# Adaptive-LayerNorm attention block on one core: the second batch is normalised by ScalarE, five heads are rotated in one piece, query weights are loaded ahead of the fourth modulation

## The chip, the cores and the metric

The kernel runs on one core of one Trainium2 chip. The metric is the device time of one launch in microseconds (us), as the median of several runs. The abbreviations are those of the profile: PE is TensorE, PEld its weight loads, DVE VectorE, ACT ScalarE, POOL GpSimd, SP SyncE, which issues nearly all DMAs. PEclk is the share of its full clock of 2.4 GHz that the throttle granted to TensorE.

## What is computed

```python
def reference(x, wq, wk, wv, wo, w12, b12, w3, b3, c, wmod):      # x: 2 x 512 x 512, 32 heads, 8 key/value heads of 128
    mod = (_silu(c) @ wmod).reshape(2, 6, 1, -1)
    sa, ca, ga, sb, cb, gb = (mod[:, 0], mod[:, 1], mod[:, 2], mod[:, 3], mod[:, 4], mod[:, 5])
    ga = (2 * (ga >= 0) - 1) * jnp.maximum(jnp.abs(ga), 0.25)
    gb = (2 * (gb >= 0) - 1) * jnp.maximum(jnp.abs(gb), 0.25)
    h = _layernorm(x, axis=-1) * (1 + ca) + sa
    x = x + ga * attention(h, wq, wk, wv, wo)      # rotary embedding on q and k, causal softmax, 4 query heads to a key head
    h = _layernorm(x, axis=-1) * (1 + cb) + sb
    return x + gb * ffn(h, w12, b12, w3, b3)       # silu(x1) * x2, then the second matrix
```

## The kernel before

Five instruction streams, one for each engine, are written out by hand. Each engine works its own stream strictly in order, and semaphores join them (`x.wait_ge(sem, n)` before an instruction, `.then_inc(sem, 1)` after one). So the order in which a function writes its calls is the order of the engine, and a waiting instruction holds up all that stands behind it.

All products are made with fp32 operands that are split into a high and a low part: one product of 128 x 512 is three matmuls per chunk of the contraction, and a projection with its four chunks is 12 matmuls (`product`, `project_k`, `project_v`, `project_q`). ACT makes the high part, POOL or DVE the low one. That holds for weights (`wq_high`, then `wq_low`), for the normalised input (`hT`), and for rotated queries and keys.

**Main part.** It has 8 key heads x 2 batches. `group` is one key head, of eight slots `s`; a slot is 128 query rows. In a slot TensorE makes the scores (four products of growing width), a query projection for a later slot (`slot_query`, into `q_bank`), sometimes a key or value projection into `x_bank`, the product of probabilities and values (`attend`) and the output product (`project_out`). DVE takes the row maxima, ACT the exponentials, DVE the reciprocal of the sums (`invert`), ACT the scaling (`normalise`), DVE the 32 x 32 transposes (`turn_blocks`), and two DMAs through DRAM lay the probabilities out for `attend`. In the first group the modulations 4, 5 and 2, which are long rows of matmuls of two columns (`modulation`), stand behind the scores of slots 1 and 2.

**Rotation.** For each projected head DVE makes two rows of products with the cosine and sine tables (`rotate`, three instructions that read the PSUM bank, then `roped`), POOL adds them (`rotated_sum`), ACT makes the high part (`rotated_high`), POOL the low part (`rotated_low`, then `rope_lo`). There are two buffers (`rope_tmp[:, n % 2]`), so rotation n waits for `rope_lo` of rotation n - 2. The first scores wait for `rope_lo` of rotations 0 (key) to 4 (query head 3); the first `slot_query` waits until rotation 5 (query head 0 of batch 1) has left its bank: `ROPE_FIRST` is 6.

**Prologue**, which the change touches. SP loads x, the two halves of modulations 0 and 1, key and query weights and the tables. TensorE makes modulations 0 and 1 as rows, and in between turns the normalised x of batch 0 into `s_banks` (`turn_x(0)`). ACT scales and shifts it (`modulate_x`), DVE splits it (`hT`), and TensorE projects key head 0 and the query heads. Batch 1 follows: DVE makes mean and reciprocal deviation (`norm_scale`, a chain of 12 instructions on 128 x 4 elements), and before the change also the normalised rows (`norm_x`, four instructions of 128 x 512); TensorE turns them (`turn_x(1)`), ACT modulates them and makes the high part, DVE the low part (`h_low`). Before the change modulation 3 stands on TensorE between the query heads 1 and 2, the norm of batch 1 on DVE between rotations, and the projection of query head 0 of batch 1 ahead of the first scores.

## Time and profile before

| | us |
|---|---|
| median of 3 runs (lowest, highest) | 840.23 (840.01, 843.87) |
| the profiled execution, its own time | 841.05 |
| its span, first to last instruction | 839.2 |
| PE busy | 790.2 (94%) |
| DVE busy | 615.1 (73%) |
| POOL busy | 560.1 (67%) |
| ACT busy | 501.9 (60%) |
| mean granted clock of TensorE | 0.969 |

A busy share is a mean over the whole span; what a change at one place is worth is read from the chain of waits there. Times in the trace count from the first instruction. Granted clock 1.00 is 2.4 GHz, 0.50 is 1.2 GHz; a stretch in between holds both.

### The profile page before, as it was taken

Reading aid. Unit: us, or ns where it says so; the run is one execution under the profiler, and the core shown is the slowest. Engines: PE = TensorE matmul, PEld = TensorE weight load, DVE = VectorE, ACT = ScalarE, POOL = GpSimd, SP = SyncE. Lnnn points to the kernel's source line nnn. Section 1 sums busy time; section 2 is a strip of 40 time slices with the busy share of each in tenths; the row PEclk is TensorE's granted clock in tenths of the full one; section 3 lists DMA queues with packets and bytes.
Section 4 is the critical chain, followed back from the end, with each engine's and each line's share of the span. In section 5 each row is a group of like instructions: output and inputs, shape, how many; then the busy total and the mean of one; then the engine's idle time right before and its main releaser. Section 6 shows DMA issues by size and latency. Waiting matters only on the chain.

```text
span 839.2 us, 11685 instructions
## 1 busy us (share of the span) xinstructions
PE 790.2 (94%) x3680; PEld 653.8 (78%) x3680; DVE 615.1 (73%) x1246; ACT 501.9 (60%) x1191; POOL 560.1 (67%) x374
## 2 busy tenths in 40 slices
PE   7989989989999999999999999999999987889887
PEld 2769868877888888888888888888888776668765
DVE  5856467867777878687768676867787778558695
ACT  2154476557667766776677667777667754853421
POOL 1453395768777877796779677989587974148552
PEclk9788799999999999999999999999999998999999
DMA  9512646677667756776676667776676854966011
GB/s 326 191 39 69 205 128 167 137 175 238 154 189 192 230 147 198 191 218 172 183 196 202 180 181 194 236 190 174 176 219 177 244 157 128 310 205 192 0 51 50
DMA packets 191885, 147.13 MB, mean 175 GB/s; under 512 B 62673, under 2 KB 168273, under 8 KB 189777
## 3 DMA queue, kind: packets, MB, share of 16 engines
q1 hardware_dynamic: 191408, 146.33, 62.3%
q8 instruction: 29, 0.48, 0.2%
q14 instruction: 32, 0.25, 0.1%
q10 hardware_dynamic: 416, 0.07, 0.0%
HBM read 91.82 MB, written 54.53 MB: 174 GB/s over the span
## 4 chain that ended last, share of the span: by engine, by line
PE 53%; POOL 13%; DVE 12%; ACT 8%; DMA 7%; SPq 4%; issue 3%; DVEq 0%; ACTq 0%; POOLq 0%
PE out_bank L571 13%; PE q_bank L504 13%; PE s_bank L504 8%; PE o_bank L557 7%; PE x_bank L504 6%; DMA spread_dram<-turned 5%; POOL pT_lo L1340 5%; POOL wo_lo_sb L1340 3%; ACT probs L1137 3%; POOL rope_tmp L1366 2%; ACT probs L1145 2%; PE o_bank L512 2%; POOL qT L1340 2%; DVE turned L827 2%; SPq L395 1%
## 5 line engine op out<-in xcount | busy, mean ns | idle before, releaser
L1340 POOL TENSOR_TENSOR pT_lo<-pT_raw,pT_hi 128x1024 fp32r<-128x1024 f32 (+1 forms) x96 | 194.7, 2043 | 87.2 <-ACT pT_hi L1114 87.2
L1137 ACT ACTIVATE probs<-probs,neg_max 128x32 f32<-128x32 f32 (+15 forms) x256 | 130.7, 512 | 181.2 <-DVE neg_max L808 181.2
L1340 POOL TENSOR_TENSOR qT<-rope_tmp,qT 128x512 fp32r<-128x512 f32 x64 | 83.3, 1301 | 101.3 <-ACT qT L1114 101.3
L827 DVE STREAM_TRANSPOSE turned<-probs 128x512 f32<-128x512 f32 (+1 forms) x64 | 96.7, 1512 | 50.5 <-DMA spread_dram<-turned 43.9
L1366 POOL TENSOR_TENSOR rope_tmp<-rope_tmp 128x512 f32<-128x512 f32 x80 | 109.3, 1373 | 29.3 <-DVE rope_tmp L785 29.3
L504 PE MATMUL s_bank<-kT,qT 128*128 128x32 f32 (+15 forms) x768 | 123.4, 309 | 4.4 <-POOL qT L1340 4.4
L504 PEld LDWEIGHTS s_bank<-kT,qT 128*128 128x128 f32 x768 | 114.5, 192 | 12.9 <-issue 4.1
L571 PE MATMUL out_bank<-wo_hi_sb,attn_hi 128*128 128x512 f32 x248 | 99.4, 401 | 15.2 <-POOL wo_lo_sb L1340 6.8
L1145 ACT ACTIVATE probs<-probs,row_inv 128x32 f32<-128x32 f32 (+15 forms) x256 | 111.9, 509 | 0.8 <-DVE row_inv L817 0.8
L808 DVE CUSTOM_DVE_ANT_0 probs<-s_bank,mask_sb 128x32 f32<-128x32 f32 (+15 forms) x256 | 98.5, 433 | 17.0 <-PE s_bank L504 16.8
L504 PE MATMUL q_bank<-hT_hi,wq_hi_sb 128*128 128x512 f32 x248 | 101.6, 410 | 1.1 <-DVE rope_tmp L785 1.0
L504 PE MATMUL q_bank<-hT_hi,wq_lo_sb 128*128 128x512 f32 x248 | 100.4, 405 | 0.0
L504 PE MATMUL q_bank<-hT_lo,wq_hi_sb 128*128 128x512 f32 x248 | 100.2, 404 | 0.0
L571 PE MATMUL out_bank<-wo_lo_sb,attn_hi 128*128 128x512 f32 x248 | 97.9, 395 | 0.0
L571 PE MATMUL out_bank<-wo_hi_sb,attn_lo 128*128 128x512 f32 x248 | 97.7, 394 | 0.0
L783 DVE TENSOR_TENSOR rope_tmp<-q_bank,cos_sb 128x512 f32<-128x512 f32 x62 | 42.5, 686 | 63.8 <-PE q_bank L504 32.6
L1114 ACT ACTIVATE pT_hi<-pT_raw 128x1024 fp32r<-128x1024 f32 (+1 forms) x96 | 83.6, 903 | 6.3 <-DMA pT_raw<-spread_dram 6.0
L557 PE MATMUL o_bank<-pT_hi,v_hi 128*128 128x512 f32 x160 | 63.7, 398 | 9.6 <-DVE attn_lo L831 8.0
L571 PEld LDWEIGHTS out_bank<-wo_hi_sb,attn_hi 128*128 128x128 f32 x248 | 47.5, 191 | 30.2 <-issue 13.4
L1340 POOL TENSOR_TENSOR wq_lo_sb<-wq_raw,wq_hi_sb 128x512 fp32r<-128x512 f32 x40 | 52.0, 1300 | 23.7 <-ACT wq_hi_sb L1114 23.7
L557 PE MATMUL o_bank<-pT_lo,v_hi 128*128 128x512 f32 x160 | 63.2, 395 | 0.0
L557 PE MATMUL o_bank<-pT_hi,v_lo 128*128 128x512 f32 x160 | 63.2, 395 | 0.0
(218 smaller groups left out, 1612.6 us busy)
## 6 DMA issues: line engine op xcount, KB each, us to landing
spread_dram<-turned SPq DMA_DIRECT2D x64, 256.0 KB, 4.1
pT_raw<-spread_dram SPq DMA_DIRECT2D x16, 1024.0 KB, 5.8
spread_dram<-turned SPq DMA_DIRECT2D x64, 192.0 KB, 5.2
pT_raw<-spread_dram SPq DMA_DIRECT2D x16, 768.0 KB, 5.0
wq_raw<-in_L_attn_wq_dram SPq DMA_DIRECT2D x36, 256.0 KB, 4.3
wo_raw<-in_L_attn_wo_dram SPq DMA_DIRECT2D x9, 1024.0 KB, 5.7
spread_dram<-turned SPq DMA_DIRECT2D x64, 128.0 KB, 4.2
pT_raw<-spread_dram SPq DMA_DIRECT2D x16, 512.0 KB, 6.0
```

Of the source, the lines that this page charges most:

```text
L504: last = pe.matmul(dst, lhs(a, cc), rhs(b, cc), start=(k == 0), stop=(k == len(todo) - 1))
L512: last = pe.matmul(o_bank[:, at:at + 2], wmod_blocks[m][:, k, n * P:(n + 1) * P], c_silu[:, :, k], start=(k == 0), stop=(k == KC - 1))
L557: last = pe.matmul(o_bank[:, :], v_s[a][:, b, st_, :], pT[bb][par][:, :, PLACES[par] - 1 - i + st_, :], start=(k == 0), stop=(k == len(ste ...
L571: last = pe.matmul(dst[:, :], attn[a][:, s % 2, h * P:(h + 1) * P], wo_s[bb][:, h, :], start=(h == 0 and (a, bb) == PARTS[0]), stop=(h == ...
L783: nc.vector.tensor_tensor(a, src[:, :], cos_sb[:, :], ALU.mult)
L808: nc.vector.tensor_tensor_reduce(prob_rows(s, t), s_banks[t][:, 0:n].rearrange("p (j s) -> p j s", s=W32), mask_sb[:, T - n:T].rearrange(" ...
L827: nc.vector.transpose(dst, src).then_inc(blocks_turned, 1)
L1114: nc.scalar.activation(dst, src, ACT.Copy).then_inc(done, 1)
L1137: nc.scalar.activation(rows, rows, ACT.Exp, bias=neg_max[:, par, t:t + 1], scale=-1.0, accum_out=row_sum[:, par, t:t + 1]).then_inc(exp_do ...
L1145: last = nc.scalar.activation(rows, rows, ACT.Copy, scale=row_inv[:, par, t:t + 1])
L1340: nc.gpsimd.tensor_tensor(dst, src, hi.bitcast(f32), ALU.subtract).then_inc(done, 1)
L1366: nc.gpsimd.tensor_tensor(a, a, b, ALU.add).then_inc(rope_sum, 1)
```

## The change

1. The norm of batch 1: `norm_scale` moves on DVE to directly behind its statistics, ahead of the split of batch 0; the four `norm_x` instructions go from DVE to ACT (as an Identity activation with scale `rstd` and bias `shift`).
2. The copy of modulations 0 and 1 out of PSUM goes from DVE to ACT.
3. SP loads query heads 1, 2, 3 and the value weights before modulation 3.
4. TensorE: `turn_x(1)` comes behind query head 1, then query heads 2 and 3, the value projection, then modulation 3. Query head 0 of batch 1 is projected into `out_bank` behind the first scores.
5. DVE: rotations 0 to 4 in one piece, then the low parts of batch 1. Rotation 5 stands in slot 0 behind `turn_blocks`.
6. ACT normalises slot 0 directly behind its exponentials; batch 1 is modulated in two pairs around the high part of rotation 2. POOL makes all weights' low parts first, then the rotations in order.

```diff
@@ SP
-            load_wq(0, 1)
+            for h in range(1, REP):
+                load_wq(0, h)
+            load_wv(0)
             load_wmod(3)
-            load_wq(0, 2)
-            load_wv(0)
-            load_wq(0, 3)
@@ TensorE, group
                     scores(g, s)
+                    if first and s == 0:
+                        pe.wait_ge(roped, 5)
+                        project_q(out_bank[:, :], 1, 0, h_lo[1])
...
-                        project_k(batch_of(v), h_lo[1] if first and s == 0 else None)
+                        project_k(batch_of(v))
@@ TensorE, prologue
             project_q(out_bank[:, :], 0, 1)
-            pe.wait_ge(mod_ready, 1)
-            modulation(3)
+            pe.wait_ge(x_normed[1], TT)
+            turn_x(1, range(KC))
             pe.wait_ge(roped, 2)
             pe.wait_ge(wq_lo, 3)
             project_q(q_bank[:, :], 0, 2)
-            pe.wait_ge(x_normed, B * TT)
-            turn_x(1, range(KC))
-            pe.wait_ge(wv_lo, 1)
-            project_v(0)
             pe.wait_ge(roped, 3)
             pe.wait_ge(wq_lo, 4)
             project_q(out_bank[:, :], 0, 3)
-            pe.wait_ge(roped, 4)
-            project_q(q_bank[:, :], 1, 0, h_lo[1])
+            pe.wait_ge(wv_lo, 1)
+            project_v(0)
+            pe.wait_ge(mod_ready, 2)
+            modulation(3)
             pe.wait_ge(h_ready[1], KC)
@@ DVE, group
                     invert(g, s)
+                    if first and s == 0:
+                        turn_blocks(g, s)
+                        first_rotation(ROPE_FIRST - 1)
@@ DVE, prologue
-            dve.wait_ge(mod_made, 2)
-            link(nc.vector.tensor_copy(mod[:, 0:2 * KC, :]..., o_bank[:, 0:4 * KC]))
-            nc.vector.tensor_scalar(one_plus[:, 0:KC, :], ...).then_inc(mod_ready, 1)
+            norm_scale(1, 2)
...
-            first_rotation(0)
-            norm_scale(1, 2)
-            first_rotation(1)
-            norm_x(1)
-            first_rotation(2)
-            first_rotation(3)
+            for n in range(ROPE_FIRST - 1):
+                first_rotation(n)
             for k in range(KC):
                 h_low(k)
-            first_rotation(4)
@@ ACT, prologue
-            act.wait_ge(mod_ready, 1)
+            act.wait_ge(mod_made, 2)
+            nc.scalar.activation(mod[:, 0:2 * KC, :]..., o_bank[:, 0:4 * KC], ACT.Copy).then_inc(mod_ready, 1)
+            nc.scalar.activation(one_plus[:, 0:KC, :]..., o_bank[:, 2 * KC:4 * KC], ACT.Copy, bias=1.0).then_inc(mod_ready, 1)
+            act.wait_ge(mod_ready, 2)
             for k in range(KC):
                 modulate_x(0, k)
             wq_high(0, 1)
+            act.wait_ge(norm_ready, 2)
+            for w in range(TT, 2 * TT):
+                nc.scalar.activation(acc[:, w, :], acc[:, w, :], ACT.Identity, bias=shift[:, w, :],
+                                     scale=rstd[:, w, :]).then_inc(x_normed[1], 1)
```

On **TensorE** around the first scores the order was this (the last matmul of query head 0 of batch 1, the scores, the first of the first slot query):

```order
L504 MATMUL q_bank<-hT_hi,wq_lo_sb 128x512
L504 MATMUL s_bank<-kT,qT 128x32 [waits rope_lo,h_ready1]
L504 MATMUL s_bank<-kT,qT 128x32 x2
L504 MATMUL s_bank<-kT,qT 128x64 x3
L504 MATMUL s_bank<-kT,qT 128x96 x3
L504 MATMUL s_bank<-kT,qT 128x128 x3
L504 MATMUL q_bank<-hT_hi,wq_hi_sb 128x512 [waits wq_lo,roped]
```

and is now this:

```order
L511 MATMUL o_bank<-c_silu,wmod_sb 128x2 [waits wmod_in3,mod_ready]
L511 MATMUL o_bank<-c_silu,wmod_sb 128x2 x15
L503 MATMUL s_bank<-kT,qT 128x32 [waits rope_lo,h_ready1]
L503 MATMUL s_bank<-kT,qT 128x32 x2
L503 MATMUL s_bank<-kT,qT 128x64 x3
L503 MATMUL s_bank<-kT,qT 128x96 x3
L503 MATMUL s_bank<-kT,qT 128x128 x3
L503 MATMUL out_bank<-hT_hi,wq_hi_sb 128x512 [waits h_lo1,roped]
...
L503 MATMUL q_bank<-hT_hi,wq_hi_sb 128x512 [waits wq_lo,roped]
```

Modulation 3 has come to stand directly ahead of the scores, and the projection of head 0 of batch 1 between the scores and the first slot query, whose wait for `roped` is unchanged.

On **DVE** behind the key's rotation (`x_bank`) the order was this:

```order
L785 TENSOR_TENSOR rope_tmp<-x_bank,sin_sb 64x512
L949 BN_AGGR moments<-stats 128x2 [waits stats_made]
L949 BN_AGGR moments<-stats 128x2 x3
L957 TENSOR_SCALAR var_eps<-moments 128x4 [waits moments_ready]
...
L963 SCALAR_TENSOR_TENSOR shift<-moments,rstd 128x4 [waits dve_chain]
L783 TENSOR_TENSOR rope_tmp<-q_bank,cos_sb 128x512 [waits q_proj]
L784 TENSOR_TENSOR rope_tmp<-q_bank,sin_sb 64x512
L785 TENSOR_TENSOR rope_tmp<-q_bank,sin_sb 64x512
L1004 TENSOR_SCALAR acc<-acc,moments,rstd 128x512 x4
L783 TENSOR_TENSOR rope_tmp<-out_bank,cos_sb 128x512 [waits rope_lo,q_proj]
```

and is now this:

```order
L785 TENSOR_TENSOR rope_tmp<-x_bank,sin_sb 64x512
L783 TENSOR_TENSOR rope_tmp<-q_bank,cos_sb 128x512 [waits q_proj]
L784 TENSOR_TENSOR rope_tmp<-q_bank,sin_sb 64x512
L785 TENSOR_TENSOR rope_tmp<-q_bank,sin_sb 64x512
L783 TENSOR_TENSOR rope_tmp<-out_bank,cos_sb 128x512 [waits rope_lo,q_proj]
```

The chain of the norm and the four wide instructions no longer stand between rotations.

On DVE **in slot 0** of the first group, from the reciprocal of the row sums on, the change gives:

```order
L817 RECIPROCAL row_inv<-row_sum 128x4 [waits exp_done]
L827 STREAM_TRANSPOSE turned<-probs 128x4x128 [waits probs_normed]
L783 TENSOR_TENSOR rope_tmp<-out_bank,cos_sb 128x512 [waits rope_lo,q_proj]
L784 TENSOR_TENSOR rope_tmp<-out_bank,sin_sb 64x512
L785 TENSOR_TENSOR rope_tmp<-out_bank,sin_sb 64x512
L783 TENSOR_TENSOR rope_tmp<-q_bank,cos_sb 128x512 [waits rope_lo,q_proj]
```

Before, rotation 5 stood ahead of the row maxima of this slot, and the transpose behind the rotation of `q_bank`. Now rotation 5, for which the slot query on TensorE waits, has maxima, reciprocal and transpose ahead of it.

## Rows read from the trace of the kernel before

**Rows 1.** Busy time by stretch: us, PE, PEld, DVE, ACT, POOL busy, granted clock, DMA.

```profile
0.00:58.47 58.47, 47.08 (x192) 31.79 (x193) 42.16 (x97) 18.05 (x33) 22.82 (x21) 0.89 0.58 192
58.47:66.14 7.67, 7.67 (x26) 6.13 (x26) 2.96 (x7) 2.89 (x10) 1.65 (x2) 0.70 0.20 59
66.14:101.60 35.46, 35.46 (x181) 32.29 (x180) 17.17 (x43) 14.80 (x40) 14.07 (x11) 0.76 0.50 145
```

**Rows 2.** The chain of waits, 26 to 67 us: start, duration, what.

```profile
26.73 0.69 DVE rope_tmp L783
...
36.52 3.72 DVE acc L1004 x4
...
53.92 0.64 ACT qT L1114
...
54.62 1.27 POOL qT L1340
...
56.03 2.64 PE s_bank L504 x12
58.67 4.88 PE q_bank L504 x12
63.56 2.74 PE x_bank L504 x12
```

**Rows 3.** Timeline of DVE, norm of batch 1: start, duration, engine, line, instruction, tiles.

```profile
29.27 0.95 DVE L957 TENSOR_SCALAR var_eps<-moments 128x4 f32<-128x4 f32 x1
...
32.74 0.16 DVE L961 SCALAR_TENSOR_TENSOR newton<-newton,var_eps 128x4 f32<-128x4 f32 x1
```

**Rows 4.** Timeline of DVE, norm of batch 0.

```profile
10.56 1.91 DVE L1004 TENSOR_SCALAR acc<-acc,moments,rstd 128x512 f32<-128x512 f32 x4
```

**Rows 5.** Timeline of ACT, norm of the second layer late in the kernel.

```profile
784.58 2.94 ACT L1197 ACTIVATE rope_tmp<-acc,shift,rstd 128x512 f32<-128x512 f32 x4 [5.94 <-DVE shift L963]
```

**Rows 6.** Timeline of POOL and DVE around the split of batch 0.

```profile
17.41 1.26 POOL L1340 TENSOR_TENSOR wq_lo_sb<-wq_raw,wq_hi_sb 128x512 fp32r<-128x512 f32 x1
...
19.81 0.43 DVE L1022 CAST hT_hi<-probs 128x512 fp32r<-128x512 f32 x1 [0.85 <-ACT probs L1180]
```

**Rows 7.** Busy time by stretch: transposes, idle PE, modulations, what followed.

```profile
13.00:15.00 2.00, 2.00 (x18) 1.79 (x18) 0.44 (x1) 0.00 (x0) 0.00 (x0) 1.00 1.13 324
18.60:21.60 3.00, 0.00 (x0) 0.00 (x0) 1.88 (x6) 2.60 (x4) 0.06 (x1) 1.00 1.09 351
...
31.90:35.50 3.60, 3.60 (x33) 3.54 (x31) 3.28 (x12) 0.00 (x0) 0.78 (x1) 1.00 0.17 15
36.50:41.80 5.30, 5.26 (x12) 4.02 (x13) 5.26 (x7) 1.67 (x3) 4.29 (x3) 0.50 0.00 0
...
52.30:56.00 3.70, 0.01 (x1) 0.00 (x0) 3.33 (x11) 0.72 (x2) 2.64 (x3) 1.00 0.29 70
56.00:62.80 6.80, 6.77 (x22) 5.88 (x23) 1.18 (x9) 3.87 (x14) 2.39 (x2) 0.51 0.28 81
...
73.50:76.40 2.90, 2.90 (x8) 2.31 (x7) 0.00 (x0) 2.81 (x6) 2.09 (x2) 0.50 0.00 0
...
80.50:89.40 8.90, 8.90 (x43) 8.90 (x44) 1.97 (x10) 5.43 (x16) 3.42 (x3) 0.50 0.74 174
...
104.00:120.00 16.00, 13.32 (x61) 10.63 (x61) 11.97 (x23) 10.68 (x26) 15.39 (x9) 1.00 0.63 185
```

**Rows 8.** Timeline of PE in slot 4 of the first group.

```profile
114.98 0.47 PE L571 MATMUL out_bank<-wo_hi_sb,attn_hi 128*128 128x512 f32 x1 [2.02 <-POOL wo_lo_sb L1340]
```

**Rows 9.** Timeline, rotation and softmax of slot 0.

```profile
41.07 0.69 DVE L784 TENSOR_TENSOR rope_tmp<-out_bank,sin_sb 64x512 f32<-64x512 f32 x1
...
59.97 1.10 ACT L1145 ACTIVATE probs<-probs,row_inv 128x32 f32<-128x32 f32 x4
...
65.72 0.71 DVE L827 STREAM_TRANSPOSE turned<-probs 128x512 f32<-128x512 f32 x1
```

**Rows 10.** Groups by line, 26 to 56 us: count, busy us, mean ns, idle before.

```profile
L991 DVE TENSOR_TENSOR hT_lo<-turned,hT_hi 128x512 fp32r<-128x512 f32 x4 | 3.7, 948 | 2.2 <-ACT hT_hi L1114 2.2
```

More of the change, by code:

```diff
@@ L173, in adaln_block @@
         stats_made, moments_ready, norm_ready = sem("stats_made"), sem("moments_ready"), sem("norm_ready")
-        x_normed, x_turned = sem("x_normed"), sem("x_turned")
+        x_normed, x_turned = [sem(f"x_normed{b}") for b in range(B)], sem("x_turned")
         h_ready, h_hi, h_lo = ([sem(f"h_{s}{b}") for b in range(B)] for s in ("ready", "hi", "lo"))
@@ L677, in _ @@
             pe.wait_ge(ident_in, 16)
[L678 removed]
+            pe.wait_ge(x_normed[0], TT)
             turn_x(0, range(KC))
@@ L876, in group @@
                             wo_low(LOAD[v - 1], n)
-                    turn_blocks(g, s)
+                    if not (first and s == 0):
+                        turn_blocks(g, s)
                     if r == 0:
@@ L1000, in _ @@
             nc.vector.tensor_tensor(c_silu[:, :, :], c_silu[:, :, :], cT[:, :, :], ALU.mult).then_inc(c_ready, 1)
-            def norm_x(b):
-                for w in range(TT * b, TT * (b + 1)):
-                    nc.vector.tensor_scalar(acc[:, w, :], acc[:, w, :], moments[:, w, 0:1], rstd[:, w, :],
-                                            ALU.subtract, ALU.mult).then_inc(x_normed, 1)
             for w in range(TT):
@@ L1011, in _ @@
             norm_scale(0, 1)
-            norm_x(0)
+            for w in range(TT):
+                nc.vector.tensor_scalar(acc[:, w, :], acc[:, w, :], moments[:, w, 0:1], rstd[:, w, :],
+                                        ALU.subtract, ALU.mult).then_inc(x_normed[0], 1)
             dve.wait_ge(x_in[2], 16)
@@ L1203, in group @@
                     exponents(g, s)
+                    if first and s == 0:
+                        normalise(g, s)
                     q_high(g, s - 1)
@@ L1210, in group @@
                             wo_high(LOAD[v - 1], n)
-                    normalise(g, s)
+                    if not (first and s == 0):
+                        normalise(g, s)
                     if first and s == 3:
@@ L1284, in _ @@
             copy_rows(1)
-            act.wait_ge(mod_ready, 1)
+            act.wait_ge(mod_made, 2)
+            nc.scalar.activation(mod[:, 0:2 * KC, :].rearrange("p m b -> p (m b)"), o_bank[:, 0:4 * KC],
+                                 ACT.Copy).then_inc(mod_ready, 1)
+            nc.scalar.activation(one_plus[:, 0:KC, :].rearrange("p m b -> p (m b)"), o_bank[:, 2 * KC:4 * KC],
+                                 ACT.Copy, bias=1.0).then_inc(mod_ready, 1)
+            act.wait_ge(mod_ready, 2)
             for k in range(KC):
@@ L1288, in _ @@
             wq_high(0, 1)
+            act.wait_ge(norm_ready, 2)
+            for w in range(TT, 2 * TT):
+                nc.scalar.activation(acc[:, w, :], acc[:, w, :], ACT.Identity, bias=shift[:, w, :],
+                                     scale=rstd[:, w, :]).then_inc(x_normed[1], 1)
             wq_high(0, 2)
+            wq_high(0, 3)
+            wv_high(0)
             rotated_high(0, 0, kT[0][0][:, :])
             rotated_high(0, 1, qT[0][0][:, :, 0, :])
-            wv_high(0)
-            wq_high(0, 3)
+            modulate_x(1, 0)
+            modulate_x(1, 1)
             rotated_high(0, 2, qT[0][0][:, :, 1, :])
-            for k in range(KC):
-                modulate_x(1, k)
+            modulate_x(1, 2)
+            modulate_x(1, 3)
             rotated_high(0, 3, qT[0][0][:, :, 2, :])
@@ L1450, in _ @@
             wk_low(0)
-            wq_low(0, 0)
-            wq_low(0, 1)
+            for h in range(REP):
+                wq_low(0, h)
+            wv_low(0)
             rotated_sum(0, 0)
-            wq_low(0, 2)
             rotated_low(0, 0, kT[0][0][:, :], kT[1][0][:, :])
-            rotated_sum(0, 1)
-            rotated_low(0, 1, qT[0][0][:, :, 0, :], qT[1][0][:, :, 0, :])
-            wv_low(0)
-            rotated_sum(0, 2)
-            wq_low(0, 3)
-            rotated_low(0, 2, qT[0][0][:, :, 1, :], qT[1][0][:, :, 1, :])
-            for n in range(3, 5):
+            for n in range(1, ROPE_FIRST - 1):
                 rotated_sum(0, n)
                 rotated_low(0, n, qT[0][0][:, :, n - 1, :], qT[1][0][:, :, n - 1, :])
-            rotated_sum(0, 5)
+            rotated_sum(0, ROPE_FIRST - 1)
             def x4_low(u):
```

6 lines of the change are left out of this document (1 added, 5 removed).

## The prediction

> **What bounds the kernel now.** I read first the busy time by stretch, to see how the prologue divides [rows 1]. From 58.47 us, the start of the first slot query, to 101.60 TensorE is never idle: 7.67 of 7.67 and 35.46 of 35.46 us busy, at a clock of 0.70 and 0.76. In the 58.47 us before it is idle for 11.4 us. So what the change does ahead of 58.47 arrives at the end through one number, the time at which the first slot query starts, and a second one, the clock at which TensorE works from there. Behind 101.60 all waits are between engines, none on a fixed time, and the whole stream shifts.
>
> The chain of waits tells what sets 58.47 [rows 2]. It runs over DVE: the first rotation at 26.73, the four wide instructions of the norm of batch 1 (3.72 us on the chain), then rotations, and over ACT and POOL for the last query head (0.64 and 1.27 us) to the scores at 56.03. TensorE does the scores in 2.64 us and the slot query in 4.88, against 2.74 for the key projection behind it, also 12 matmuls. The difference, 2.14 us, is the clock: 0.51 in the stretch from 56.00 to 62.80 [rows 7].
>
> The timelines give the prices. A small instruction of the norm chain takes 0.16 us alone and 0.95 where a POOL instruction runs [rows 3]. The four wide ones took 1.91 us for batch 0, with POOL idle [rows 4], and 3.72 on the chain for batch 1 [rows 2]. ACT normalises four rows of the same size in 2.94 us [rows 5].
>
> **The change, part by part.** I follow the new order from the split of batch 0.
>
> *Norm chain moved forward on DVE.* It now starts when the statistics are done, near 17.0 us, and its first small instruction meets POOL's 17.41 to 18.67 [rows 6]; then 12 at some 0.2 us with their gaps: 21.0. The split of batch 0 started at 19.81 [rows 6], so it is 1.2 us late. Part of it comes back, since the same split waited for POOL once anyway and ACT's modulation will then be ahead. Bounds for the end of the key projection are 0 and 1.2 us late; I take 0.6, as neither end is nearer: its rotation starts at 27.3 instead of 26.73. ACT takes over two copies of modulations, which cost what DVE's did: nothing.
>
> *Norm on ACT.* 2.94 us [rows 5], from 22.5 to about 25.5, under the projections of key and query head 0. Its cover is the time until `turn_x(1)` at 32.7; seven us are left. The weights' high parts wait behind it, query head 2's until 26, used at 34.7. *Loads reordered:* query and value weights come earlier, modulation 3's megabyte later, but it is used 11 us later: nothing either way.
>
> *TensorE's own work.* From 27.3: query heads 0 and 1, 2 x 2.74; transposes 2.0 [rows 7]; heads 2 and 3 and the value projection, 3 x 2.74; modulation 3, 3.6 [rows 7]. That is 13.7 + 2.0 + 3.6 = 19.3 us, so 46.6, if nothing stalls it and the clock stays at 2.4 GHz.
>
> *The rotations.* Head 3 is projected at 40.2. Its rotation is 3 x 0.69 = 2.1 us [rows 9], to 42.3. POOL needs 1.27 for the sum, ACT 0.64, POOL 1.27, with handoffs 3.3: 45.6 if POOL is free. But POOL must first make sum and low part of head 2, to about 43.0, and shares the time with DVE's four low parts, which took 3.7 us for four with POOL beside them, where 2.8 would do at 0.69 each [rows 10, 9]. So the last low part lands at 43.0 + 3.3 + 1.0 = 47.3. This is behind TensorE's 46.6, so **the scores start at 47.3** instead of 56.03, 8.7 us earlier. Bounds: 46.6 and 49.5.
>
> The Trainium skill (SBUF — State Buffer, "Who interferes with whom") says that a Vector instruction with two SBUF inputs and a GpSimd one exclude each other for their whole length. Rows 3 agree. By that rule the four low parts could put up to 4 x 0.69 = 2.8 us between POOL's instructions where I put 1.0; the scores would start at 49.1 and the sum below would gain 1.8 us less.
>
> *Query head 0 of batch 1 behind the scores.* This is the price of the change. The first slot query still waits for rotation 5, and rotation 5 now stands behind maxima, reciprocal and transpose. Modulation 3 now directly precedes the scores; before, the stretch behind it ran at 0.50 [rows 7], and the scores took 2.64 us at that level [rows 2]. I take the same: scores end at 49.9. From the end of the scores to ACT's scaling there were 59.97 - 58.67 = 1.3 us, the scaling takes 1.10, the transpose 0.71 [rows 9]: 53.0. TensorE meanwhile projects head 0 of batch 1: at 1.2 GHz 4.9 us, at 2.4 GHz 2.74. Low stretches behind such a place lasted some 6.8 us [rows 7], so the level rises near 54: the head ends at 54.7. It ends last, not the softmax. Rotation 5: 2.1. **The first slot query starts at 56.9**, 1.6 us before 58.47, of the 8.7 that had been won. TensorE is idle from 54.7 to 56.9 for it.
>
> *Clock behind it.* The slot query took 4.88 us at 0.51. If the level is 2.4 GHz by then, it takes 2.74: 2.14 less. An idle of 2.02 us on TensorE [rows 8] did not lower the level, 1.00 in its stretch; idles of 3.0 and 3.7 us did [rows 7]. The 2.2 us here are nearest to the first. So I take 2.14.
>
> **Sum.** 1.6 + 2.1 = 3.7 us. Against the profiled execution, 841.05, that is 837.35; it stands 0.8 above the median, so the forecast for the median of 840.23 is **836.5 us**. 0.5% of it, 4.2 us, is about what a measurement of this kernel can tell from no change; the border is 836.0.
>
> **The rivals.**
>
> *B, the clock falls at the new idle.* The 2.2 us at 54.7 to 56.9 do what 3.0 us did [rows 7]. The slot query then takes 4.9 us again: the gain is 1.6 and the time 838.6. For it: idle of that length lies between the two cases that rows show, and the transition may come at another point of the program in each execution. Against: rows 8.
>
> *C, the clock does not fall at the scores.* Before, TensorE was idle 1 us behind modulation 3; now 0.7 at most. Scores take 1.5 us, the head 2.74; rotation 5 then follows the softmax, at 54.3 or so, and the slot query starts 1.8 us sooner: 834.7. Against: the fall behind the other modulations too, with no idle at all (0.50 from 73.50 and from 80.50) [rows 7].
>
> *D, transposes.* The Trainium skill (TensorE: Matmul & The Clock Gate, Part 4, "PE-mode transpose") says that transposes do not count as work that keeps the clock up. The row from 13 to 15 us is 16 transposes at 1.00 [rows 7], though the clock may have been about to fall. As a mechanism of this kernel: `turn_x(1)` now stands between projections, query head 2 and part of head 3 run at 1.2 GHz, and 1.7 us (half of a low stretch such as the one around 73.50 to 76.40) is lost on a path where 0.7 us is slack; DVE's and POOL's chain hangs on the same heads, so 1.7 us less is won: 838.2.
>
> *E, slower than before.* The level falls at the idle as in B and is still 1.2 GHz when modulation 4 begins, near 66 us. Modulation 4 then runs as the later ones did, 43 matmuls in 8.9 us, 0.21 each [rows 7], so 6.8 for 32 instead of 3.5: 3.3 lost. Key projection and the next query head run low in part, 3 more. From B's 838.6 that gives 844.9. It decides from the point at which the level is low when modulation 4 starts; before, it had risen at 62.8, 5.8 us ahead. Against: dense projections have always brought it back before [rows 1, 7].
>
> *F, nothing arrives.* The scores start late (49.5, the upper bound) and the clock falls as in B; or the loads do hold something. 840.0.
>
> **How the numbers follow.** A, the forecast, 0.45; B 0.20; C 0.14; D 0.05; E 0.07; F 0.09. A has its own width: bounds of the key projection (-0.6 to +0.6) and of the scores' start (-0.7 to +2.2) give 835.2 to 838.7. Below 836.0 lie C, a third of A and the best of B and D, where modulations 4, 5 and 2 happen to lose less clock: 0.14 + 0.16 + 0.05 = 0.35. Over 844.4 lies most of E: 0.06. Between: 0.59. The range has to reach C at the low end, less its outermost, and F at the other: 833.8 to 840.6 leaves out E, part of C and of F, near 0.18.
>
> **What would show it.** In the changed profile: the norm chain of batch 1 at 17 to 21 us, the key's rotation from 27.3; ACT's four normalising instructions of 0.73 us each; TensorE without idle from 27 to 46.6; the first scores at 47.3 (46.6 to 49.5) with a clock near 0.5; head 0 of batch 1 ending at 54.7, then some 2.2 us idle on TensorE, released by DVE's rotation; the slot query at 56.9 and of 2.74 us; slot 1's scores starting near 62.4 instead of 66.14. The forecast is wrong if TensorE's busy stretch does not begin earlier, if it begins before 55, or if the clock between it and 101.60, shifted, differs from 0.76: then the phases of modulations 4, 5 and 2 decide, not the prologue.

## The result, and the profile after

| | before | after |
|---|---|---|
| median of 20 runs each, on the same chips (lowest, highest) | 841.69 (836.95, 844.52) | 836.84 (833.23, 840.01) |
| the profiled execution, its own time | 841.05 | 836.97 |
| its span | 839.2 | 834.4 |
| PE busy | 790.2 | 789.0 |
| DVE busy | 615.1 | 609.1 |
| ACT busy | 501.9 | 505.0 |
| POOL busy | 560.1 | 560.0 |
| mean granted clock | 0.969 | 0.970 |

The ratio of the runs is 0.9946, 95% interval 0.9932 to 0.9961: 3.3 to 5.7 us less, 4.9 between the medians. The predicted time of 836.5 is met within 0.4 us. Part of that is luck: the forecast took 3.7 us off the 840.23 of three runs, and twenty runs put the kernel before at 841.69, so 4.9 were won and not 3.7. The way there is another one too, and that is what the rest is about. A single execution far above its kernel at a clock far below it (one of 982.64 us at 0.743, for example) is left out of all figures.

Busy time by stretch of the changed kernel, from the three borders of [rows 1] at the same matmuls (start of the first slot query, of slot 1's scores, and the matmul that stood at 101.60), and then the low stretches. Columns as in rows 1: stretch, us, busy of PE, PEld, DVE, ACT, POOL, granted clock, DMA share, GB/s.

```profile
0.00:59.87 59.87, 49.90 (x193) 33.62 (x193) 38.72 (x95) 23.01 (x46) 21.44 (x20) 0.86 0.60 194
59.87:67.04 7.17, 7.17 (x25) 5.76 (x25) 2.06 (x3) 1.15 (x2) 3.13 (x3) 0.76 0.28 77
67.04:99.30 32.26, 32.26 (x182) 29.34 (x181) 16.97 (x42) 14.83 (x41) 13.86 (x11) 0.84 0.48 143
24.00:30.80 6.80, 6.08 (x15) 4.48 (x15) 3.95 (x7) 3.18 (x6) 4.17 (x4) 0.52 1.05 387
47.90:58.10 10.20, 9.78 (x33) 8.09 (x33) 5.28 (x20) 2.83 (x12) 1.45 (x1) 0.52 0.20 52
61.60:65.00 3.40, 3.40 (x11) 2.65 (x9) 0.69 (x2) 0.76 (x2) 1.27 (x1) 0.56 0.02 5
82.10:92.30 10.20, 10.20 (x37) 9.03 (x37) 0.32 (x2) 4.12 (x12) 2.53 (x2) 0.52 0.88 264
```

The first slot query starts at 59.87, 1.4 us **later** than the 58.47 of before, and slot 1's scores at 67.04 instead of 66.14. At 99.30 the kernel is ahead, by 2.3 us: the stretch from slot 1's scores took 32.26 us instead of 35.46, at a clock of 0.84 instead of 0.76, and with the same matmuls. So in this execution the prologue brings no earlier start of slot 1.

The chain of waits of the changed kernel, 25 to 67 us (start, duration, what), against [rows 2]:

```profile
25.12 4.21 PE x_bank L503 x9
29.32 3.34 PE q_bank L503 x12
...
37.14 2.74 PE q_bank L503 x12
39.87 2.72 PE out_bank L503 x12
...
45.31 4.48 PE o_bank L511 x32
49.80 2.66 PE s_bank L503 x12
52.46 5.24 PE out_bank L503 x12
...
59.87 4.39 PE q_bank L503 x12
64.25 2.94 PE x_bank L503 x12
```

From 25 us to 57.7 the chain is TensorE's own work, as the new order wants. The scores come 6.4 us earlier (49.66 against 56.03 on the timeline), but head 0 of batch 1 behind them takes 5.24 us, at half clock, then rotation 5 is waited for, and the slot query takes 4.39. The timeline of DVE (start, duration, engine, line, instruction, idle before and its releaser):

```profile
18.38 1.21 DVE L961 TENSOR_SCALAR var_eps<-moments 128x4 f32<-128x4 f32 x1
...
22.95 1.51 DVE L1021 CAST hT_hi<-probs 128x512 fp32r<-128x512 f32 x1
...
29.44 0.69 DVE L783 TENSOR_TENSOR rope_tmp<-x_bank,cos_sb 128x512 f32<-128x512 f32 x1 [2.83 <-PE x_bank L503]
...
44.76 5.14 DVE L995 TENSOR_TENSOR hT_lo<-turned,hT_hi 128x512 fp32r<-128x512 f32 x4
```

The timeline of ACT:

```profile
22.69 2.93 ACT L1292 ACTIVATE acc<-acc,shift,rstd 128x512 f32<-128x512 f32 x4
```

The timeline of POOL:

```profile
18.30 1.26 POOL L1347 TENSOR_TENSOR wq_lo_sb<-wq_raw,wq_hi_sb 128x512 fp32r<-128x512 f32 x1
22.89 1.29 POOL L1347 TENSOR_TENSOR wq_lo_sb<-wq_raw,wq_hi_sb 128x512 fp32r<-128x512 f32 x1 [3.32 <-ACT wq_hi_sb L1107]
...
47.81 1.53 POOL L1347 TENSOR_TENSOR qT<-rope_tmp,qT 128x512 fp32r<-128x512 f32 x1 [0.74 <-ACT qT L1107]
```

The four rows cost ACT 2.93 us, as read from [rows 5]. DVE's first small instruction of the norm and one CAST of the split each stand beside a POOL instruction and take 1.21 and 1.51 us. Without POOL beside them a small instruction took 0.16 and a CAST 0.43 [rows 3, 6].

**A measure that takes the clock out.** The times of one kernel lie 7 to 11 us apart, and the low stretches fall at other places from one execution of the change to the next. Span and mean granted clock are known for every execution. Span x clock, which I call order, is what the execution would have lasted had TensorE's clock been full, if a low stretch costs exactly the half speed; span x (1 - clock) is what the low clock took. For the kernel before, span x clock has a standard deviation of 1.6 us where the times have 2.6. For 95 executions of the kernel before, beside the experiments, the means are 811.3 and 28.1; for 29 of the changed one 809.1 and 25.3. So of 5.1 us of gain some 2.3 (standard error 0.4) are order, and 2.8 (0.6) are clock.

It is an approximation, since an idle engine loses nothing to the clock, and it takes out too much: among the 95 executions a us more of low-clock loss goes with only 0.7 us more of time. By that slope 2.0 us would be clock and 3.1 order. Differences of a few tenths in these columns are therefore not to be read.

**The same at one place.** Busy time up to slot 1's scores, columns as above, in the first profile of before, the change's first and second, and *norm parts only* (both described below):

```profile
0.00:66.14 66.14, 54.75 (x217) 37.91 (x217) 45.12 (x104) 20.94 (x42) 24.47 (x23) 0.87 0.54 176
0.00:67.04 67.04, 57.07 (x217) 39.39 (x217) 40.78 (x98) 24.16 (x48) 24.58 (x23) 0.85 0.56 182
0.00:64.59 64.59, 55.26 (x217) 37.80 (x218) 40.71 (x98) 24.05 (x48) 24.50 (x23) 0.87 0.58 189
0.00:64.41 64.41, 54.75 (x217) 36.82 (x217) 38.82 (x98) 24.14 (x48) 23.96 (x23) 0.87 0.56 181
```

Three of them have the same clock, 0.87, and there slot 1 starts 1.6 and 1.7 us earlier than before. With half of the low time taken off, the change's first profile is 0.8 us ahead too. So a part of the order gain does come out of the prologue; the first profile hides it under more low clock.

### The profile page after: what moved, and what is told of

Read it like the earlier page. It is cut to its first block, busy times and chain, and to the rows that moved or that the text cites. A ratio compares the mean times of both kernels' runs of the same rounds, so it can differ in the third digit from the quotient of the medians.

```text
span 834.4 us, 11685 instructions
## 1 busy us (share of the span) xinstructions
PE 789.0 (95%) x3680; PEld 651.7 (78%) x3680; DVE 609.1 (73%) x1240; ACT 505.0 (61%) x1197; POOL 560.0 (67%) x374
## 4 chain that ended last, share of the span: by engine, by line
PE 54%; POOL 12%; DVE 12%; DMA 7%; ACT 7%; SPq 5%; issue 3%; DVEq 0%; ACTq 0%; POOLq 0%
PE out_bank L570 13%; PE q_bank L503 13%; PE s_bank L503 8%; PE o_bank L556 7%; PE x_bank L503 6%; DMA spread_dram<-turned 5%; POOL pT_lo L1347 4%; ACT probs L1130 3%; POOL wo_lo_sb L1347 2%; PE o_bank L511 2%; ACT probs L1138 2%; DVE turned L827 2%; SPq L341 2%; POOL rope_tmp L1373 2%; POOL qT L1347 2%
## 5 line engine op out<-in xcount | busy, mean ns | idle before, releaser
L503 PE MATMUL q_bank<-hT_hi,wq_hi_sb 128*128 128x512 f32 x244 | 98.6, 404 | 2.4 <-DVE rope_tmp L785 2.2
L503 PE MATMUL q_bank<-hT_hi,wq_lo_sb 128*128 128x512 f32 x244 | 97.5, 400 | 0.0
L503 PE MATMUL q_bank<-hT_lo,wq_hi_sb 128*128 128x512 f32 x244 | 97.2, 398 | 0.0
L570 PEld LDWEIGHTS out_bank<-wo_hi_sb,attn_hi 128*128 128x128 f32 x248 | 47.3, 191 | 28.4 <-issue 12.7
L1347 POOL TENSOR_TENSOR wq_lo_sb<-wq_raw,wq_hi_sb 128x512 fp32r<-128x512 f32 x40 | 51.9, 1299 | 25.4 <-ACT wq_hi_sb L1107 25.4
```

The lines of the kernel that those rows point to most:

```text
L503: last = pe.matmul(dst, lhs(a, cc), rhs(b, cc), start=(k == 0), stop=(k == len(todo) - 1))
L570: last = pe.matmul(dst[:, :], attn[a][:, s % 2, h * P:(h + 1) * P], wo_s[bb][:, h, :], start=(h == 0 and (a, bb) == PARTS[0]), stop=(h == ...
L1347: nc.gpsimd.tensor_tensor(dst, src, hi.bitcast(f32), ALU.subtract).then_inc(done, 1)
```

## The experiments

Theories at the outset: **T1**, the prediction's: the earlier prologue moves the slot query and a full clock at it brings the rest; **T2**, the idle ahead of the slot query lowers the clock there (rival B), and the gain arises behind it. The first expectations put the question as P (the prologue is faster, and the first profile was unlucky) and K (the prologue is not faster by itself, and the low clock only lies at cheaper places). Later runs divide what T2 leaves open. Ratios are to the kernel before on the same chip.

| kernel | median (runs) | ratio [95%] | span x clock | lost to clock |
|---|---|---|---|---|
| change, again | 835.29 (9) | 0.9927 [0.9901, 0.9953] | 809.1 | 24.6 |
| before, again | 841.94 (10) | 1.0013 [0.9988, 1.0037] | 811.4 | 28.2 |
| no wait for rotation 5 | 832.08 (6) | 0.9899 [0.9860, 0.9937] | 807.2 | 24.1 |
| the same, again | 834.38 (9) | 0.9913 [0.9886, 0.9940] | 807.1 | 25.3 |
| chain behind the split | 837.22 (11) | 0.9967 [0.9933, 1.0001] | 811.3 | 24.9 |
| rows on DVE | 837.05 (12) | 0.9948 [0.9924, 0.9973] | 810.7 | 24.7 |
| norm parts only | 835.98 (12) | 0.9939 [0.9910, 0.9968] | 808.8 | 25.8 |
| idle filled | 834.59 (12) | 0.9931 [0.9904, 0.9957] | 807.7 | 25.3 |
| dense for modulation 3 | 832.21 (6) | 0.9888 [0.9849, 0.9928] | 808.1 | 21.7 |
| both | 834.96 (12) | 0.9927 [0.9903, 0.9952] | 807.7 | 25.8 |
| modulations together | 840.66 (12) | 0.9987 [0.9963, 1.0011] | 809.7 | 29.1 |
| modulation 3 in slot 1 | 845.68 (12) | 1.0037 [1.0012, 1.0062] | 812.7 | 30.7 |

**The change, again.** No edit.

> The changed kernel once more, unchanged, to see what of its profile repeats. In its first profile the first slot query starts at 59.87 us, 1.4 us later than the 58.47 of before, and the 4.8 us that its span is shorter by arise behind it, in steps at 73 to 83 us, near 690 and near 745. Theory P (the prologue is faster, this one profile was unlucky): the first slot query starts at 57 to 58 us here. Theory K (the prologue is not faster by itself; the clock of TensorE is low at other, cheaper places): it starts at 59 to 60 again, and the level is low for about 10 us around the first scores again. Both: ratio to before 0.992 to 0.997.

Timeline of PE in this second profile of the same kernel:

```profile
47.67 2.49 PE L503 MATMUL s_bank<-kT,qT 128*128 128x32 f32 x12 [0.72 <-POOL qT L1347]
...
57.38 0.50 PE L503 MATMUL q_bank<-hT_hi,wq_hi_sb 128*128 128x512 f32 x1 [2.19 <-DVE rope_tmp L785]
...
64.59 2.66 PE L503 MATMUL s_bank<-kT,qT 128*128 128x416 f32 x12
```

The prologue can be 2 to 2.5 us faster than in the first profile. The idle ahead of the slot query is the same 2.19 us, released by rotation 5, and the clock falls again, at 58.0: the slot query needs 57.38 to 61.83. From slot 1's scores to the third border (columns as above) the clock is that of before:

```profile
64.59:100.07 35.48, 35.48 (x182) 32.26 (x181) 16.98 (x42) 14.83 (x41) 14.05 (x11) 0.76 0.44 130
```

It takes 35.48 us at 0.76, where before took 35.46 at 0.76. So the start of slot 1, 1.6 us earlier, passes on to the border unchanged, as the prediction says of such a gain. The two executions of the change, 2.5 us apart at slot 1, are 0.8 apart the other way at the border. P's landmark is met (57.38); K's low clock around the scores is there too (6.8 us, then 3.4 more at the slot query).

**The kernel before, again.** No edit; the control.

> The kernel before once more, unchanged, for a second profile of it. The prologue's waits should repeat: scores at 55.5 to 56.5 us, first slot query 2.4 us behind, low clock in the stretches behind modulation 3, behind the idle at 52 to 56, and around modulations 4, 5 and 2. What differs by more than 1 us from the first profile by 101 us, or in the last 170 us, is the spread of the clock between executions and no effect of a kernel.

The scores stand at 55.94 and the low stretches within 0.3 us of where they were in the first profile. The two profiles of the kernel before agree there; the two of the change do not.

**No wait for rotation 5.** The first slot query writes `q_bank`, which rotation 3 leaves; rotation 5 reads `out_bank`. So it need wait for four rotations only.

```diff
-            def slot_query(g, s):
+            def slot_query(g, s, first=False):
...
-                need(pe, roped, ROPE_GROUP, g, ROPE_FIRST + rope_q_at(s) - (1 if s % TT == 1 else 0))
+                if first and s == 0:
+                    pe.wait_ge(roped, 4)
+                else:
+                    need(pe, roped, ROPE_GROUP, g, ROPE_FIRST + rope_q_at(s) - (1 if s % TT == 1 else 0))
...
-                        slot_query(g, s)
+                        slot_query(g, s, first)
```

> The first slot query writes q_bank, whose last reader is rotation 3; here it waits for that (roped 4) and not for rotation 5. Theory P: TensorE's idle of 2.2 us ahead of the slot query goes, and with it the second fall of the clock; 2 to 4 us less than the changed kernel. Theory K: the idle goes, but the clock falls somewhere else; 0 to 2 us less. Rival (DVE is the limit there): the wait moves to the key projection or the next scores, and nothing is won.

> The kernel that waits for four rotations, a second time, for a narrower interval. If the wait for rotation 5 costs about 3 us, as its first run showed (832.08 against 835.29 of the change alone), the median is 831 to 833.5; if that was the luck of few executions, 835 to 837. Landmark: the scores of slot 1 near 60.7 us, against 66.2 to 67.0 with the wait.

Timeline of PE, first of the two profiles:

```profile
47.92 2.47 PE L503 MATMUL s_bank<-kT,qT 128*128 128x32 f32 x12 [0.73 <-POOL qT L1350]
...
55.28 0.40 PE L503 MATMUL q_bank<-hT_hi,wq_hi_sb 128*128 128x512 f32 x1
...
60.73 2.66 PE L503 MATMUL s_bank<-kT,qT 128*128 128x416 f32 x12
```

The idle is gone, the slot query starts at 55.28 at full clock, and slot 1's scores at 60.73 (61.86 in the second profile) against 64.59 and 67.04. Both sets of runs are below the change's medians; together their span x clock is 807.1 against 809.1. The wait costs 1.9 us of order (standard error 0.5). Of the 2.7 to 6.3 us by which slot 1 starts earlier in the profiles, part is the second low stretch, and it comes back later. This is the best kernel of the study that computes all of the reference, 0.9 to 1.0% faster than the kernel before.

**Chain behind the split.** The norm's small chain goes behind the split of batch 0 on DVE, and the high parts of the remaining weights ahead of the four rows on ACT.

```diff
@@ DVE
-            norm_scale(1, 2)
             for k in range(KC + 1):
...
+            norm_scale(1, 2)
@@ ACT
+            wq_high(0, 2)
+            wq_high(0, 3)
+            wv_high(0)
             act.wait_ge(norm_ready, 2)
...
-            wq_high(0, 2)
-            wq_high(0, 3)
-            wv_high(0)
```

> The 12 small instructions of batch 1's norm go behind the split of batch 0 on DVE, where it is idle for 2.8 us during the key projection; on ACT the weights' high parts go ahead of the four normalised rows. If the early chain is what delayed the key projection (split at 21.7 instead of 19.8), the projection ends near 27.5 instead of 29.3 and the scores start up to 1.8 us earlier; time 1 to 3 us less. If the late end of the key projection came of the clock (low for 6.8 us from 24.0) and of the later landing of x, nothing moves by more than 0.5 us.

Timeline of DVE:

```profile
19.65 0.43 DVE L1020 CAST hT_hi<-probs 128x512 fp32r<-128x512 f32 x1 [2.65 <-ACT probs L1174]
...
22.53 3.45 DVE L1023 TENSOR_TENSOR hT_lo<-probs,hT_hi 128x512 fp32r<-128x512 f32 x2
...
26.31 0.83 DVE L961 TENSOR_SCALAR var_eps<-moments 128x4 f32<-128x4 f32 x1
27.18 1.20 DVE L962 TENSOR_SCALAR rstd<-var_eps 128x4 int32<-128x4 int32 x1
...
30.27 0.69 DVE L783 TENSOR_TENSOR rope_tmp<-x_bank,cos_sb 128x512 f32<-128x512 f32 x1
```

The split starts 2 us earlier, but two low parts take 3.45 us beside three POOL instructions in a row (22.22 to 27.12), and two small instructions stand beside POOL again. The key's rotation begins at 30.27, no earlier than in the change, and its span x clock is that of the kernel before. What the prediction had called the price of the early chain is not saved by moving the chain: it meets POOL there too.

**Rows on DVE.** DVE makes the four normalised rows of batch 1 behind the split, instead of ACT.

```diff
@@ DVE
+            for w in range(TT, 2 * TT):
+                nc.vector.tensor_scalar(acc[:, w, :], acc[:, w, :], moments[:, w, 0:1], rstd[:, w, :],
+                                        ALU.subtract, ALU.mult).then_inc(x_normed[1], 1)
@@ ACT
-            act.wait_ge(norm_ready, 2)
-            for w in range(TT, 2 * TT):
-                nc.scalar.activation(acc[:, w, :], ...).then_inc(x_normed[1], 1)
```

> The four rows of batch 1 are normalised by DVE again, but behind the split and ahead of the first rotation, where DVE is idle for 2.8 us. If ACT's part matters by itself, the time goes up by 1 us or more. If only the place between the rotations had mattered, DVE does the rows in 2 to 4 us (POOL runs beside them), the first rotation starts up to 1 us later at most and the time is that of the changed kernel within 1 us.

Timeline of DVE:

```profile
27.79 3.84 DVE L1028 TENSOR_SCALAR acc<-acc,moments,rstd 128x512 f32<-128x512 f32 x4
31.55 0.68 DVE L783 TENSOR_TENSOR rope_tmp<-x_bank,cos_sb 128x512 f32<-128x512 f32 x1
```

They cost DVE 3.84 us beside POOL, as in [rows 2], and the key's rotation is at 31.55; scores 50.95, slot query 59.88. The scores are 3.3 us later than in the change's second profile, but some 1.7 of that is a low clock at 8 us, at TensorE's first matmuls, which the other profile does not have. In span x clock this kernel is 1.7 us behind the change (standard error 0.6): giving the rows to ACT is worth about that.

**Norm parts only.** The kernel before with parts 1 and 2 of the change (early chain, rows and copy of the modulations on ACT) and nothing of parts 3 to 6.

```diff
@@ DVE
+            norm_scale(1, 2)
             for k in range(KC + 1):
...
             first_rotation(0)
-            norm_scale(1, 2)
             first_rotation(1)
-            norm_x(1)
...
@@ ACT
...
             wq_high(0, 1)
+            act.wait_ge(norm_ready, 2)
+            for w in range(TT, 2 * TT):
+                nc.scalar.activation(acc[:, w, :], ...).then_inc(x_normed[1], 1)
```

> The kernel before with the norm of batch 1 alone changed (chain early on DVE, rows and the copy of modulations on ACT); TensorE's and SP's order and the rotations' places as before. If the norm between the rotations is what held the first scores at 56.03 (3.7 us of rows and 2.4 to 5 us of chain), they start at 50 to 52 us and the time is 2 to 4 us below before, about all of the change's gain. If the wait moves to the rotations' chain on DVE, POOL and ACT or to the projection that stands ahead of the scores, they start at 53 to 55 and less than 2 us are won.

Timeline of PE:

```profile
55.93 2.11 PE L504 MATMUL s_bank<-kT,qT 128*128 128x32 f32 x12 [2.92 <-POOL qT L1342]
57.84 0.73 PE L504 MATMUL q_bank<-hT_hi,wq_hi_sb 128*128 128x512 f32 x1
```

Busy time by stretch of the same kernel, columns as above:

```profile
0.00:55.90 55.90, 46.27 (x180) 29.54 (x181) 35.18 (x85) 20.30 (x34) 21.22 (x21) 0.88 0.61 199
55.90:62.00 6.10, 6.07 (x26) 5.29 (x27) 1.29 (x10) 3.84 (x14) 2.40 (x2) 0.72 0.31 90
...
66.00:97.30 31.30, 31.30 (x169) 28.32 (x168) 15.43 (x40) 13.89 (x38) 13.12 (x10) 0.78 0.54 155
```

The scores stand at 55.93, against 56.03, and the whole gain of the change is there: 835.98, span x clock 808.8 against 809.1. But the equal place of the scores is an accident of this profile. TensorE's first matmuls of the modulations fell on a low clock, in *norm parts only* (first line) and not in the kernel before (second line):

```profile
8.59 5.29 PE L662 MATMUL q_bank<-wmod_sb,c_silu 128*2 128x512 f32 x8 [2.31 <-DMA wmod_sb<-in_L_wmod_dram]
7.81 3.59 PE L662 MATMUL q_bank<-wmod_sb,c_silu 128*2 128x512 f32 x8 [1.77 <-DMA wmod_sb<-in_L_wmod_dram]
```

They took 1.7 us longer, and the key projection starts at 24.00 instead of 21.66. From there to the scores it is 31.9 us instead of 34.4, so the moved norm shortens the prologue by some 2.4 us, of which up to 0.7 may be clock (8.8 us of low clock on the way against 10.2). At slot 1's scores 1.7 us of it are left, at the same mean clock.

The stretch from the scores to 62 us runs at 0.72, where the one from 56.00 to 62.80 before had 0.51 [rows 7]. For T1 this means: an earlier prologue does bring something, but parts 3 to 6, which bring scores that are six to eight us earlier, add nothing that these runs can tell. The wait for rotation 5, which part 5 puts behind the softmax, takes it away again; *no wait for rotation 5* has 1.6 us of order more than this kernel (standard error 0.6).

**Idle filled.** Nine matmuls of 512 columns, whose result nobody reads, in the idle ahead of the slot query.

```diff
                         project_q(out_bank[:, :], 1, 0, h_lo[1])
+                        pe.wait_ge(v_turned, 1)
+                        for _ in range(9):
+                            pe.matmul(x_bank[:, :], wk_s[0][:, 0, :], hT[0][:, 0, T:2 * T], start=True, stop=True)
```

> The changed kernel, with nine matmuls of 512 columns whose result is not used put into TensorE's idle of 2.2 to 2.8 us ahead of the first slot query. If that idle makes the clock fall (low again from 58.0 and 61.6 in two profiles of the changed kernel), the fall goes: the slot query takes 2.7 to 3.3 us and the time is 1 to 2 us less, though no work is gone. If the fall has another cause, slot query and time stay as they are.

Windows of this kernel:

```profile
56.00:66.00 10.00, 9.87 (x46) 8.03 (x45) 6.15 (x10) 1.15 (x2) 4.14 (x4) 1.00 0.40 114
66.00:102.00 36.00, 35.34 (x173) 31.59 (x171) 15.98 (x41) 16.40 (x44) 14.17 (x11) 0.72 0.42 123
```

With the idle filled the clock does not fall at the slot query, as T2 wants: 1.00 from 56 to 66, slot 1's scores at 63.37. The other profiles bear it out: in four with no idle ahead of the slot query (both of *no wait for rotation 5*, *both* and *modulations together*) the clock does not fall there either, while of the six with 2.18 us or more it falls in five. So it was the idle. But the time, 834.59, can't be told from the change's, and from 66 to 102 the clock is 0.72 in this profile. So rival B's price at the place, some 2 us, is real, and what is won there was in this execution lost again where modulations 4, 5 and 2 run. Its span x clock is 1.4 us below the change's (standard error 0.5), which I can't explain.

**Dense for modulation 3.** Sixteen matmuls of 512 columns stand in for modulation 3's 32 slots of two columns; the shift of the second norm is left out by this.

```diff
             pe.wait_ge(mod_ready, 2)
-            modulation(3)
             pe.wait_ge(h_ready[1], KC)
+            for _ in range(16):
+                last = pe.matmul(o_bank[:, :], wk_s[0][:, 0, :], hT[0][:, 0, 0:T], start=True, stop=True)
+            last.then_inc(mod_made, 1)
```

> The changed kernel, with modulation 3 (32 matmuls of 2 columns, 3.6 us) replaced by 16 matmuls of 512 columns, also 3.6 us; the shift of the second norm is left out. If modulation 3 is what lowers the clock around the first scores, they take 1.5 us instead of 2.5 and the head behind them 2.7 instead of 4.3 to 5.2: the first slot query starts 1.5 to 3 us earlier. If the low stretch comes of the short matmuls of the scores themselves, it stays, only later by some us, and the time by less than 1 us.

Timeline of PE:

```profile
44.42 3.79 PE L706 MATMUL o_bank<-hT_hi,wk_hi_sb 128*128 128x512 f32 x16
48.73 1.55 PE L503 MATMUL s_bank<-kT,qT 128*128 128x32 f32 x12 [0.52 <-POOL qT L1349]
...
56.15 0.69 PE L503 MATMUL q_bank<-hT_hi,wq_hi_sb 128*128 128x512 f32 x1 [3.07 <-DVE rope_tmp L787]
```

Same busy time ahead of the scores, same wait for POOL, and the scores take 1.55 us at full clock instead of 2.5. So modulation 3 lowers the clock at the scores, and not the short idle. It is one profile, but in all of the others in which modulation 3 stands ahead of the scores the clock falls during it or within 1.5 us behind it. The head then ends early, TensorE waits 3.07 us for rotation 5, and the clock falls there. Lost to clock: 21.7 us, the least of all kernels (standard error 1.3).

**Both.** The edits of *no wait for rotation 5* and of *chain behind the split* together.

> Waits for four rotations, and the norm chain of batch 1 stands behind the split on DVE, with all weights' high parts ahead of the rows on ACT. Each alone: 832.1 and 837.8. If the costs add, this is 833.5 to 835.5 (slower than without the moved chain); if the slower one was so only by the clock behind the scores, both are equal at 831 to 833.

834.96 beside 834.38 on the same chip, 807.7 beside 807.1: no difference that these runs can tell, where the chain's place had seemed to cost 2.2 us of order with the wait in place. Why it should cost less without that wait stays open.

**Modulations together.** *No wait for rotation 5*, and modulation 3 directly ahead of modulation 4.

```diff
@@ prologue
-            modulation(3)
@@ group
                     if first and s == 1:
+                        modulation(3)
                         modulation(4)
```

> Waits for four rotations, and modulation 3 stands behind the scores of slot 1, directly ahead of modulation 4, so that no modulation precedes the first scores. If the low clock at the scores comes from modulation 3 ahead of them, scores take 1.5 us and head 0 of batch 1 2.8 us, both at full clock, but 16 more products of two columns stand in slot 1 and the low clock behind modulations 3, 4, 5 and 2 is the same or longer: 829 to 832 if the low time at the scores (6.8 us, so 3.4 lost) is saved, 832 to 834 if it only moves to the other modulations. The scores start no earlier than 47 us either way, since POOL's low parts set them; TensorE idles some 3.5 us ahead of them, and if that idle lowers the clock by itself, the scores still take 2.5 us.

Timeline of PE:

```profile
48.74 2.39 PE L503 MATMUL s_bank<-kT,qT 128*128 128x32 f32 x12 [4.20 <-POOL qT L1350]
...
64.09 11.66 PE L511 MATMUL o_bank<-c_silu,wmod_sb 128*128 128x2 f32 x64
```

A miss: 840.66, over six us more than forecast. The idle ahead of the scores is 4.20 us, and it lowers the clock by itself, so the scores gain nothing. The two modulations take 11.66 us where modulation 4 alone takes 3.63 in the kernel without this edit; modulation 3's 3.6 us had been free in the prologue, under POOL's last low part.

**Modulation 3 in slot 1.** The same move in the change as it is.

> The change with modulation 3 behind the scores of slot 1 alone (the wait for rotation 5 as in the change). Head 0 ends by 52.5 at full clock and the wait for rotation 5 then has nothing to hide under: slot query near 55.5 to 56.5, and 2 to 3.5 us idle ahead of it, which lowers the clock. If the gain of the change hangs on where the slot query starts, 833 to 835; if on the clock around modulations 4, 5 and 2, it is 836 to 838.

Window of this kernel:

```profile
66.00:102.00 36.00, 36.00 (x181) 33.22 (x180) 11.95 (x28) 12.05 (x31) 9.33 (x7) 0.67 0.36 110
```

845.68, slower than the kernel before. Slot 1's scores start at 64.77, where the change's second profile has 64.59: the slot query waits for rotation 5 either way (57.57). All of the loss is behind: the clock is 0.67 from 66 to 102 us. I had expected 838 at most. The place of modulation 3 that the change chose, under a wait for POOL, is right.

## Why the prediction was right in its number, and where it was not

- **Early chain on DVE.** Forecast: from 17.0 to 21.0 us, split 1.2 us late, key rotation at 27.3. Measured in the first profile: 18.38 to 21.76, with the statistics of batch 1 starting at 15.46 instead of 14.56, and the split 1.9 us late (1.0 in the second); the rotation at 29.44 and 28.20. The step that failed is "part of it comes back": in the first profile a CAST met POOL (1.51 us), and the low stretch at the key projection, 3.4 us long before (22.1 to 25.5), was now 6.8 (24.0 to 30.8 at 0.52), 4.21 us for nine of its matmuls.
- **Rows on ACT**, 22.5 to 25.5: 22.69 to 25.62. Right, and *rows on DVE* shows that they matter.
- **TensorE dense, scores at 47.3**, bounds 46.6 to 49.5: 49.66, 47.67, and 47.92 to 49.05 in three profiles of other kernels with the same prologue. Late by the key projection's delay; the mechanism (POOL's last low part, 0.7 us behind modulation 3) is right where the prologue was fast. The four low parts took 5.14 us, not 3.7, so the Trainium skill's rule (SBUF — State Buffer, "Who interferes with whom") was nearer for the four instructions. The 49.1 it gave for the scores lies within what was measured, but 47.67, with a key rotation 0.9 us later than forecast, does not need it. Rows 3, which the prediction calls in agreement, were no test of it: their instruction reads one tile, not two.
- **Scores at half clock, 2.64**: 2.80 and 2.49. *Dense for modulation 3* shows the cause. Rival C is out, and so is D: query heads 2 and 3 behind the transposes took 2.74 and 2.72 us, full speed. The Trainium skill's sentence on transposes (TensorE: Matmul & The Clock Gate, Part 4) shows no effect here.
- **Idle of 2.2 us for rotation 5**: 2.19, exactly.
- **"The first slot query starts at 56.9"**: 59.87 and 57.38. This term of 1.6 us is gone: on average it starts when it did before. It inherits the key projection's delay, and in the first profile the low stretch lasted 10.2 us where I had taken 6.8.
- **"The 2.2 us here are nearest to the first. So I take 2.14."** Wrong: the slot query took 4.39 and 4.45 us. The clock fell at the idle in both profiles of the change, and *idle filled*, with the four profiles that have no idle there, shows that it was the idle. That is rival B, to which I had given 0.20. B's 838.6 and the 1.6 us of the late start would have made 840.2.
- **Sums.** Rival C does not add up: from its own rows the scores end at 48.8, the transpose at 51.9 and rotation 5 at 54.0, which is 2.9 us before 56.9 and not 1.8. The upper end of A's width takes in one of its two bounds (838.7; with both 839.3). Neither changes the forecast.
- **The time all the same.** The sum was a slot query that starts 1.6 us earlier and takes 2.1 us less. The runs show about 0 (59.87 and 57.38, against 58.47) and 0.5 (4.39 and 4.45, against 4.88). By slot 1's scores the change is 0.9 us late in one profile and 1.6 early in the other, where the forecast had 3.7 early. What it had not counted is that the low clock takes another share of the whole span from one kernel to the other: 2.8 us less on average, beside 2.3 us of order (2.0 and 3.1 by the slope). The sign "if the clock between it and 101.60, shifted, differs from 0.76" came in one profile (0.84) and not in the other (0.76). *Norm parts only* has order and clock without parts 3 to 6. The number was right and its working was not.

What stays open: of the 2.3 us of order, 0.8 and 1.6 stand at slot 1's scores in the change's two profiles, and 1.7 in that of *norm parts only*. For the rest, and for the clock's 2.8 us, I can name no single wait and no place.

## What to carry to other kernels

An edit that brings a stage forward is worth what its last waiter gains: find which semaphore value that waiter asks for, and whether it needs it; here one that asked for two rotations too many cost about 1.9 us of order, and with it the reordering of parts 3 to 6 brought nothing that could be told. Put long rows of tiny matmuls under a wait that exists anyway: on the path, the same 32 matmuls cost 6 to 10 us here. And where the clock changes level at other places in each execution, judge an edit by span x clock over many executions beside the time, knowing that it takes out somewhat too much, since a single profile's stretch can show 2 us that the next one takes back.

## What the runs showed of the hardware

- An idle of 2.19 us on TensorE was followed by a fall of the clock for 3.4 us (means of 0.56 and 0.53 in these stretches of the change's two profiles), and in four of the five profiles that have this idle; in *rows on DVE* it was not. One of 2.02 us was not either [rows 8].
- Behind sixteen matmuls of 512 columns in 3.79 us and 0.52 us of idle the clock stayed at 1.00 (*dense for modulation 3*). With modulation 3's 32 matmuls of two columns ahead of the scores it fell in each profile, with no idle behind them (the change's first profile), 0.72 us (its second) and 2.47 us (*both*).
- Low stretches at the first matmuls of the modulations, near 8 us, stand in six of the fourteen profiles, and not in the other profile of the same kernel where there are two (*no wait for rotation 5*). Where they stand, eight matmuls took 5.29 us instead of 3.59, so the place of scores is compared between two profiles only with this in view.
- DVE beside POOL: one CAST of 0.43 us took 1.51, two low parts of 0.69 took 3.45, and small instructions of 0.16 took 0.83 and 1.20 in a row. The CAST and the first small instruction of the norm have one input, so this is not confined to instructions with two.
- Executions of one program lie 7 to 11 us apart. For the kernel before, span x clock spreads less (1.6 us against 2.6), so much of it is how much of the span the low stretches take; for the changed one it does not (1.7 against 1.8).
